# First sequence's query and key packing of a masked cross attention, moved into the drain of the mixing stage before it

## What is computed

```python
x = _layernorm(x + _L0_attn_ref(x, ...))            # time mixing and channel mixing
x = _layernorm(x + _L0_xattn_ref(x, ctx_1024, ctx_1024, mask_1x1xSxS2_ik0, ...))
x = _layernorm(x + _L0_ffn_ref(x, ...))             # 7 experts, 2 per row, and a shared one
...
# _L0_attn_ref, its second half (the first one is a recurrence over time, with three products)
x = x + jnp.einsum('btd,cd->btc', rwkv, Wo)
g = _ln(x, ln2_g, ln2_b)
gg = _tshift(g)
gk = g * fm_k + gg * (1 - fm_k)
gr = g * fm_r + gg * (1 - fm_r)
kf = jnp.square(jax.nn.relu(jnp.einsum('btc,fc->btf', gk, Fk)))     # 256 to 1024
kv = jnp.einsum('btf,cf->btc', kf, Fv)                              # 1024 to 256
x = x + jax.nn.sigmoid(jnp.einsum('btc,dc->btd', gr, Fr)) * kv
# _L0_xattn_ref: 16 heads of 16 features, B = 16, S = 256
Q = proj(q, w_q, b_q); K = proj(k, w_k, b_k); V = proj(v, w_v, b_v)
scores = jnp.einsum('bhqd,bhkd->bhqk', Q, K) / math.sqrt(dk)
scores = jnp.where(mask == 0, jnp.float32(-1000000000.0), scores)
attn = jax.nn.softmax(scores, axis=-1)
x = jnp.einsum('bhqk,bhkd->bhqd', attn, V)
return x.transpose(0, 2, 1, 3).reshape(B_, S_, D) @ w_o.T + b_o
```

## Time and profile before

| | us |
|---|---|
| median of 3 runs (2710.52, 2714.11, 2725.44) | 2714.11 |
| the profiled execution's own time | 2720.61 |
| its span, first to last instruction | 2719.0 |
| PE busy | 2439.2 (90%), 18357 products |
| DVE busy | 1889.6 (69%) |
| ACT busy | 1136.9 (42%) |
| POOL busy | 1009.4 (37%) |
| mean granted TensorE clock, as a share of full speed | 0.951 |

### The profile page before, as it was taken

The page is one execution under the profiler, slowest core; times in us unless marked ns, Lnnn a source line. Parts: engine busy times, 40 slices in busy tenths (PEclk is TensorE's granted clock), DMA queues, the critical chain, the costliest instruction groups (busy, mean ns, idle before and its releaser), DMA issues. The chain is left out here.

```text
span 2719.0 us, 52464 instructions
## 1 busy us (share of the span) xinstructions
PE 2439.2 (90%) x18357; PEld 2038.8 (75%) x18358; DVE 1889.6 (69%) x5094; ACT 1136.9 (42%) x2089; POOL 1009.4 (37%) x1423
## 2 busy tenths in 40 slices
PE   3999998899999699999999999997987899996697
PEld 2787786466666399999999999996865566664692
DVE  6999993476776557666676666665865588887464
ACT  2655654355555322222122222221473565663462
POOL 3545553111111155324552453311112145555672
PEclk7999999899999799999999999998988999998899
DMA  3334100322322020001312022103101335330428
GB/s 105 102 119 137 59 1 16 83 72 79 113 77 53 17 101 27 29 33 66 120 31 71 29 72 73 35 26 122 55 1 43 83 102 143 87 84 3 133 87 317
DMA packets 164245, 204.33 MB, mean 75 GB/s; under 512 B 21059, under 2 KB 138350, under 8 KB 164080
## 3 DMA queue, kind: packets, MB, share of 16 engines
q1 hardware_dynamic: 132992, 152.31, 18.8%
q0 software_dynamic: 15648, 23.70, 2.7%
q10 hardware_dynamic: 15440, 26.22, 2.6%
HBM read 95.76 MB, written 75.45 MB: 63 GB/s over the span
## 5 line engine op out<-in xcount | busy, mean ns | idle before, releaser
L1831 PE MATMUL m_gu<-m_x_hi,m_w_hi 128*128 128x256 f32 x1632 | 461.8, 283 | 17.3 <-issue 10.4
L1831 PE MATMUL m_gu<-m_x_lo,m_w_hi 128*128 128x256 f32 x1632 | 457.1, 280 | 0.0
L1831 PE MATMUL m_gu<-m_x_hi,m_w_lo 128*128 128x256 f32 x1632 | 457.0, 280 | 0.0
L1868 ACT ACTIVATE m_sg<-m_gu 128x256 f32<-128x256 f32 x408 | 156.7, 384 | 660.9 <-PE m_gu L1831 660.9
L1904 DVE TENSOR_TENSOR m_h<-m_sg,m_gu 128x256 f32<-128x256 f32 x408 | 171.4, 420 | 251.4 <-ACT m_sg L1868 249.7
L1249 ACT ACTIVATE x_pt<-x_ps 128x1024 f32<-128x1024 f32 x256 | 261.9, 1023 | 180.5 <-PE x_ps L1010 175.0
L1831 PEld LDWEIGHTS m_gu<-m_x_hi,m_w_hi 128*128 128x128 f32 x1632 | 310.6, 190 | 21.4 <-issue 11.8
L1831 PEld LDWEIGHTS m_gu<-m_x_lo,m_w_hi 128*128 128x128 f32 x1632 | 308.8, 189 | 0.0
L1831 PEld LDWEIGHTS m_gu<-m_x_hi,m_w_lo 128*128 128x128 f32 x1632 | 308.6, 189 | 0.0
L1386 DVE CUSTOM_DVE_ANT_0 x_ps<-x_ps,x_mb 128x256 f32<-128x256 f32 x512 | 201.5, 456 | 113.4 <-PE x_ps L1010 113.4
L1820 PE MATMUL m_yp<-m_w_hi,m_h_hi 128*128 128x256 f32 x816 | 237.8, 291 | 4.4 <-DVE m_h_lo L1906 4.3
(11 more groups left out here) (333 smaller groups left out, 5566.2 us busy)
## 6 DMA issues: line engine op xcount, KB each, us to landing
yt<-zero SPq DMA_DIRECT2D x8, 2048.0 KB, 10.6
x_kpack<-x_kh SPq DMA_DIRECT2D x128, 128.0 KB, 3.1
x_qpack<-x_qh SPq DMA_DIRECT2D x128, 128.0 KB, 3.0
m_yr<-yt SPq DMA_DIRECT2D x16, 1024.0 KB, 17.6
m_x<-xs SPq DMA_DIRECT2D x36, 258.0 KB, 2.6
xs<-zero SPq DMA_DIRECT2D x8, 1072.0 KB, 5.8
m_x<-xs SPq DMA_DIRECT2D x32, 268.0 KB, 3.0
c_cx<-in_ctx SPq DMA_DIRECT2D x32, 256.0 KB, 3.4
```

The costliest lines, as they stand in the source:

```text
L1831: ins = pe.matmul(gu[:, m % 4, n, :], wp[n][:, c, m * P:m * P + P], xp_[:, c, :], start=(c == 0 and k == 0), stop=(c == KC - 1 and k == 2))
L1868: act.activation(sg[:, m % 4, :], gu[:, m % 4, 0, :], ACT.Silu).then_inc(silu_ready, 1)
```

## The change

During half 17 of the mixing stage each engine now also does a part of sequence 0's work for the cross attention:

- ACT turns the K weight at the half's head (`cross_rows`), copies the transposed rows, and at the half's end writes K and Q in full and rounded (`cross_keep`, 4 instructions each).
- DVE turns the Q weight at the half's head (`cross_weights`) and makes the mask at its end (`cross_mask`, 6 instructions).
- PE transposes the rows of sequence 0 and makes K behind `time_output` (`cross_keys`), and Q behind `channel_gate` (`cross_queries`), in banks K and V.
- POOL sets the ones at the half's head and makes the two low parts at its end.
- SP issues the 12 packing transfers, and waits for them before the stage ends.

The results lie in the dead tiles inv, y1, sr (K in full, rounded, low), ev, y2, difh (Q) and q (transposed rows). The packs of sequence 0 go to `first_packs`, which shares its memory with `raw`, a buffer that is loaded only in the middle of the cross attention. Weights for V, the output and the router are now loaded by `load_cross` too. In the cross attention, period 0 becomes `masked_first`, and sequence 0's V product moves into it. `fill` is issued there 14 times in place of 28. The ones and zeros of `x_vp` are written by POOL in place of DVE. The layer-1 cross attention keeps its code.

```diff
@@ rwkv_stage
+            sp.wait_ge(cross.ones_ready, 1)
+            sp.wait_ge(cross.kh_ready, 1)
+            pack_part(sp, kpack, 0, cross_kh, cross.pack_loaded)
+            pack_part(sp, kpack, 2, cross_kh, cross.pack_loaded)
...
+            sp.wait_ge(cross.pack_loaded, 16 * PACK_DMAS)
             sp.wait_ge(padded, 16 * 2 * STEPS)
...
+            def cross_ones():
+                pool.wait_ge(rw_ready, B)
+                pool.memset(kpack.bitcast(F32), 1.0).then_inc(cross.ones_ready, 1)
...
+            def cross_keys():
+                pe.wait_ge(x1_ready, 1)
+                for t in range(TB):
+                    for c in range(KC):
+                        ins = pe.transpose(bank(V)[:, c, t * P:t * P + P], st.res[:, t, c * P:c * P + P], st.ident[:])
+                ins.then_inc(cross.t_ready, 1)
+                pe.wait_ge(cross.cx_loaded[0], 16)
+                pe.wait_ge(cross.wk_turned, 1)
+                project(K, cross.wqk[:, 1], cross.cx[:, 0]).then_inc(cross.k_ready, 1)
+
+            def cross_queries():
+                pe.wait_ge(cross.wq_turned, 1)
+                pe.wait_ge(cross.xT_ready, 1)
+                project(V, cross.wqk[:, 0], cross_xT).then_inc(cross.q_ready, 1)
...
                 at(b, time_output)
+                if half == LAST:
+                    cross_keys()
                 at(a, keys_gates_values)
                 at(c, channel_gate)
+                if half == LAST:
+                    cross_queries()
                 at(b, turn2)
...
+            def cross_mask():
+                dve.wait_ge(cross.mask_loaded, 64)
+                for n in range(3):
+                    for t in range(TB):
+                        dve.tensor_scalar(cross.mb[:, n, t, :], cross.mi[:, n, t, :], 0, NEG, ALU.is_equal,
+                                          ALU.mult).then_inc(cross.mask_ready, 1)
@@ xattn_stage
-            turn_in(0)
-            project_keys(0)
-            project_queries(0)
-            project_values(0)
+            if not EARLY:
+                turn_in(0)
+                project_keys(0)
+                project_queries(0)
+                project_values(0)
+
+            def masked_first():
+                query_scores(0, 0)
+                turn_in(1)
+                fill(0, 2)
+                query_scores(0, 1)
+
+                project_queries(1)
+                query_scores(0, 2)
+
+                project_keys(1)
+                query_scores(0, 3)
+
+                project_values(0)
+                fill(0, 2)
+                query_scores(0, 4)
+
+                project_values(1)
+                fill(0, 2)
+                query_scores(0, 5)
+
+                fill(0, 4)
+                query_scores(0, 6)
+
+                fill(0, 4)
+                query_scores(0, 7)
...
+            if EARLY:
+                pool.memset(vp[:, :, :, :, DH:32], 0.0).then_inc(vp_preset, 1)
+                pool.wait_ge(vp_preset, 1)
+                pool.memset(vp[:, :, :, :, DH:DH + 1], 1.0).then_inc(vp_preset, 1)
...
+            def masked_first():
+                for g in range(4):
+                    maxima(0, g)
+                values(0)
+                maxima(0, 4)
+                maxima(0, 5)
+                values(1)
+                maxima(0, 6)
+                maxima(0, 7)
```

More of the change, by code:

```diff
@@ L744, in xattn_stage, with pack_of @@
         qpack, kpack = sb("qpack", [P, PACKS, HPC, S], F32R), sb("kpack", [P, PACKS, HPC, S], F32R)
+        def pack_of(which, n):
+            if n < EARLY:
+                return st.first_packs[:, which]
+            return (kpack, qpack)[which][:, n % PACKS]
+        KEYS, QUERIES = range(2)
         vp = sb("vp", [P, PACKS, TB, HEADS, 32])
@@ L966, in turn_in @@
             def turn_in(n):
-                if n:
+                if n > EARLY:
                     pe.wait_ge(vp_ready, n)
-                if n == 1:
+                if n == 1 and not EARLY:
                     pe.wait_ge(kh_ready, 1)
@@ L1009, in scores @@
                     here, blk = slice(64 * (k // 2), 64 * (k // 2) + depth), 2 * j + k % 2
-                    ins = pe.matmul(bank(first + k // 2)[:, k % 2, :], left[here, n % PACKS, blk, t * P:t * P + P],
-                                    moving[here, n % PACKS, blk, :], start=not mask, stop=not mask or k % 2 == 1)
+                    ins = pe.matmul(bank(first + k // 2)[:, k % 2, :], pack_of(left, n)[here, blk, t * P:t * P + P],
+                                    pack_of(moving, n)[here, blk, :], start=not mask, stop=not mask or k % 2 == 1)
                 return ins
@@ L1562, in open_period @@
                 at(q, maxima, 7)
-            for p in PERIODS:
-                if masked:
+            for p in PERIODS[EARLY:]:
+                if EARLY and p == 0:
+                    masked_first()
+                elif masked:
                     masked_period(p)
```

233 lines of the change are left out of this document (152 added, 81 removed).

## The result

| | before | after |
|---|---|---|
| median of the runs, us | 2714.11 (2710.52 to 2725.44, 5 runs) | 2694.13 (2693.95 to 2707.88, 5 runs) |
| ratio after/before | | 0.9937, 95% interval 0.9916 to 0.9957 |
| span of the profiled execution | 2719.0 | 2706.2 |
| mean granted clock | 0.951 | 0.951 |
| first scores of sequence 0 | 483.69 | 465.12 |

(The five runs of before are the three shown above and two made beside after.) The median fell by 20.0 us, 0.74%; by the ratio of runs side by side it is 0.63%, 17.1 us. The forecast was 16.5 us, 0.61%. It was right, and the interval (11.7 to 22.8 us) takes it in.

The account below looks back on a forecast made before the run. No engine's total was taken to decide; the serial 39.0 us at the cross attention's start did. Period 0 -16.6 and drain +0.1 gave -16.5 us, from a median of 2714.1 to 2697.6 us, 80% range 2688 to 2709.

Parts of the forecast that it names:

- Where the gain comes from: Cross attention's start: turning weights, Q, K and packs of sequence 0, 18.4 us in series, now end before the barrier.
- Period 0: Cross attention's start to the transpose of the first maxima, rebuilt from eight groups' pitches: 22.4 us against 39.0, 16.6 gained.
- The wait for ACT in group 2: Period 0: K of sequence 1 waits 1.7 us until ACT has kept Q, so the group takes 3.4 us.
- The clock: Behind the stage border: PE starts at 1.2 GHz and dense work brings 2.4 GHz back at about 471.5.
- Granted clock 0.5 beyond 475: Cross attention's start: a slow clock (1.2 GHz) still granted after 475 would show the forecast wrong.
- Rival 1: Period 0: slow clock stays through groups 1 to 4, 7.9 us more, gain 8.6, time 2705.5; chance 0.14.
- The drain: End of the mixing stage: PE's inserted transposes and two projections cost +0.1 us, with ends 0 and +4.1.
- The cover of 3.92 us: PE's free time from `time_output` to `turn2` in the drain, against 3.9 to 4.1 us of new work.
- I take 0: Drain: delay of `turn2` if DVE's mask and POOL's 1/sqrt exclude each other; 0 taken, up to 1.3 us.
- Border, packs, first key scores: Signs of being right: stage border at 464.8 within 0.3, packs landed by 453, first key scores 16.5 us earlier.
- Rival 3: Period 1 keeps the fast clock, and its 2.3 us over period 2 go too; time 2695.3; chance 0.07.
- Sum: Whole kernel: -16.6 at the cross attention's start, +0.1 in the drain, -16.5 us; median 2697.6 us.

Follow-up runs that it names:

- e3: Changed kernel, but SP issues sequence 0's 12 packing transfers only when the mixing stage's last rows are written; 2718.03 us, ratio 1.0013 to the kernel before.
- e1: Changed kernel without any filler products in period 0 (14 taken out); 2698.62 us, ratio 0.9945 to the kernel before.
- e4: Changed kernel with DVE's mask made one half later, where POOL is idle; 2699.40 us, ratio 0.9941 to the kernel before.
- e6: Changed kernel with PE's two inserted projections in the drain (K and Q) made twice each; 2706.68 us in 1 run.
- e7: Changed kernel with the mask one half later and sequence 0's V product ahead of sequence 1's K in period 0; 2693.30 us, ratio 0.9919 to before.
- e8: e7 with 5 fillers in period 1 as well; 2694.53 us, ratio 0.9925 to the kernel before.
- e5: Changed kernel with the six mask instructions back behind the border, ahead of DVE's first maxima; 2707.77 us, ratio 0.9984 to the kernel before.

## Why the prediction was right, step by step

- **Where the gain comes from**: latencies in series at the start, packing transfers above all. Right, and e3 shows it for the transfers by putting them back (11.4 of 15.8 us). The other 4.4 us are not divided. A part of them is the clock's second fall, which is gone. The prediction had its price in the row of a projection at 1.2 GHz, but did not name it as a gain.
- **Period 0**: forecast 22.4, measured 22.78. By groups, forecast and measured: 2.8 and 2.62, 3.9 and 4.16, 3.4 and 3.72, 2.7 and 2.79, 2.7 and 2.79, 2.2 and 2.23, 2.2 and 2.24, 2.5 and 2.23. The wait for ACT in group 2, forecast 1.7, was 1.32. Building a stage anew from pitches of rows held to 0.4 us in the sum and 0.3 in each group. That the sum is so close is in part luck: the same code takes 21.8 to 23.1 us, by when the clock returns.
- **The clock**: taken to return at about 471.5. Measured 0.95 for 471 to 477. "Granted clock 0.5 beyond 475", named as a sign of failure, was put too widely: period 0 has none there, but period 1 opens at the slow clock (3.78 us for a projection), as it did before. Rival 1 (the clock returns late) did not come, and e1 shows that the return doesn't hang on the fillers.
- **The drain**: forecast +0.1, measured +0.33. The cover of 3.92 us was read rightly, though the two waits in the rows add up to 3.50 only: in e4 some 3.9 us of new work on PE move `turn2` by nothing, and e6 shows the cover used up. The term that was off is "I take 0" for the mask beside POOL's 1/sqrt: it was 0.33, between the ends of 0 and 1.3 that the text gave, and e4 takes it away whole. The rule of the Trainium skill cited there ("SBUF — State Buffer", section "Who interferes with whom") pointed the right way. The 1.3 worked out with it was four times too high here, since only three of POOL's small instructions were hit, by 0.15, 0.04 and 0.13 us.
- **Border, packs, first key scores**: border 464.51 (forecast 464.8, within 0.3), the packs there by 451.6 (453), key scores 16.67 earlier (16.5). Right, though the first two are times from the start of the span, and this execution was already 0.6 us early at `quotient`; from there the border came 0.34 later than before. POOL's presets for sequence 1 ended at 472.16 (472.5).
- **Rival 3** (period 1 keeps its clock): did not come, 27.0 against 27.2. e7 and e8 show what a part of it is worth, 1.6 and 2.9 us.
- **What the prediction did not see**: the mask was costed by DVE's idle time alone, as work that could stand in either place at 1.3 us. In the new cross attention POOL's presets stand at its start, and e5 shows that the mask beside them would have cost 7.3 us. So nearly half of the 15.8 us would be lost with the mask there and POOL's presets not held back. That the sum came out right without naming this is luck. In before the same mask took 1.30 at 469.09, when POOL's first preset was over (467.7).
- **Sum**: chain -15.8 in place of -16.5; the two medians differ by 20.0, and by ratio 17.1 (11.7 to 22.8). What the median gave beyond the chain can't be told from scatter.

## What to carry to other kernels

When the next stage starts with a chain of latencies (project, copy, pack by small transfers) and the stage before it drains, count the drain's waits on PE and put just that much work into them; what pays is the transfers' time, so start those earliest. Place DVE's `tensor_scalar` work and POOL's long presets at different times, since here the two side by side lengthened the chain by 7.3 us, and one after the other by 0.9. And compare landmarks, not spans: a stage that is 16 us shorter showed as 12.8 us in the profile and 20.0 in the medians.

## What the runs showed of the hardware that was not expected

- Six mask instructions of 128x256 took 7.15 us beside POOL's presets (three of 128x2048, 1.9 us each, and one of 128x1536), and 1.30 us where POOL waited. Three of them took 2.0 to 2.1 us each in place of 0.286. Beside the same mask, two of POOL's 2-element operations took 0.35 and 0.24 in place of 0.20, and its power 0.83 in place of 0.70.
- The same code at the opening of the cross attention took 21.8 to 23.1 us, and all of the difference was when the clock came back during its first projection (2.49 to 3.78 us).
- A loop with a period of 25.6 us of nearly gapless PE work has, in some executions, one fall of the granted clock per period to 0.5, for about 3.5 us, at the same place each time, and then takes 27.3. Between none and nine of its twelve periods were hit. Three fillers of 128x512 ahead of the place prevent it and cost 0.7 us a period.
